# Softmax denominators of the first attention layer: sums of probability tiles moved to GpSimd, denominators formed after the next unit's first key tile

## The reference

```python
def _L0_conv_ref(x, w_proj, b_proj, w_out, b_out):
    B, C, H, W = x.shape                      # 8, 256, 32, 32
    N = H * W                                 # 1024 tokens
    tokens = x.reshape(B, C, N).transpose(0, 2, 1)
    qkv = (tokens @ w_proj + b_proj).reshape(B, N, 8, 3 * 32)
    q, k, v = jnp.split(qkv, 3, axis=-1)
    attn = jnp.einsum('bihd,bjhd->bijh', q, k) * 32 ** (-0.5)
    attn = jax.nn.softmax(attn, axis=2)
    res = jnp.einsum('bijh,bjhd->bihd', attn, v).reshape(B, N, 256)
    out = res @ w_out + b_out + tokens
    return out.transpose(0, 2, 1).reshape(B, C, H, W)
```

## Time and profile before

| what | value |
|---|---|
| time, median of 3 runs | 3152.33 us (3150.02 to 3154.6) |
| the profiled execution | 3150.14 us, its span 3148.4 us |
| mean granted TensorE clock, of full speed | 0.929 |
| PE / DVE / ACT / POOL busy | 85% / 70% / 41% / 21% |
| layer 0's four units in the fourth image | 1233.5 to 1360.5 us |

### The profile page before, as it was taken

One profiled execution on the slowest core, in us unless ns is written; L12 is line 12 of the kernel. 1 busy time (PEld: TensorE's weight loads), 2 busy tenths in 40 slices (PEclk: granted clock), 3 DMA queues, 4 the chain that ended last, 5 costly groups with the idle time before them and its releaser, 6 DMA issues.

```text
span 3148.4 us, 43492 instructions
## 1 busy us (share of the span) xinstructions
PE 2668.8 (85%) x14974; PEld 1865.5 (59%) x14974; DVE 2200.9 (70%) x2403; ACT 1287.3 (41%) x1860; POOL 656.9 (21%) x405
## 2 busy tenths in 40 slices
PE   6889979899788897888879888888888898888993
PEld 4447754577545775467654676447764477644772
DVE  4776668666686676867678566785668766777666
ACT  2553325433354333543335333453334533255333
POOL 0520116102160022500225002340024300252011
PEclk8999989999899998999989999899989999999997
DMA  6100050000400004000040001300022000310016
GB/s 151 27 24 1 0 128 1 24 1 14 115 1 24 1 14 115 1 24 1 23 106 1 24 1 42 87 1 24 1 64 65 24 1 1 92 38 24 1 54 240
DMA packets 46389, 124.58 MB, mean 40 GB/s; under 512 B 9792, under 2 KB 21312, under 8 KB 42560
## 3 DMA queue, kind: packets, MB, share of 16 engines
q1 hardware_dynamic: 46144, 121.41, 14.1%
HBM read 43.01 MB, written 23.86 MB: 21 GB/s over the span
## 4 chain that ended last, share of the span: by engine, by line
PE 59%; issue 13%; DVE 11%; ACT 4%; SPq 4%; POOL 4%; DMA 3%; DVEq 0%; ACTq 0%; POOLq 0%
PE tile L1352 23%; PE pv L1352 10%; POOL acc L619 4%; PE tile L1611 4%; PE tile L1430 4%; PE tile L1456 3%; SPq L518 3%; PE pv L1466 3%; DVE small L961 3%; PE tile L1486 2%; DMA stack<-qk_r 2%; PE tile L1633 2%; PE tile L1741 2%; PE tile L1660 1%; PE tile L1511 1%
## 5 line engine op out<-in xcount | busy, mean ns | idle before, releaser
L961 DVE TENSOR_REDUCE small<-tile 128x1 f32<-128x1024 f32 x512 | 598.3, 1216 | 116.9 <-PE tile L1430 116.7
L740 ACT ACTIVATE p<-tile 128x512 f32<-128x512 f32 (+1 forms) x640 | 411.0, 684 | 247.4 <-PE tile L1456 246.0
L1430 PE MATMUL tile<-stack 96*128 96x512 f32 x1024 | 368.1, 451 | 118.4 <-DVE small L961 45.6
L1352 PE MATMUL tile<-qk_r 128*128 128x512 f32 x1536 | 377.9, 395 | 0.0
L1430 PEld LDWEIGHTS tile<-stack 96*128 96x128 f32 x1024 | 180.5, 201 | 319.7 <-DVE small L961 111.8
L619 POOL TENSOR_TENSOR acc<-acc,p 128x1024 f32<-128x1024 f32 x144 | 359.1, 2518 | 1.9
L649 POOL TENSOR_TENSOR row_sum<-act 128x256 f32<-128x256 f32 x32 | 42.1, 1335 | 1498.3 <-DVE act L1187 1498.3
L1352 PEld LDWEIGHTS tile<-qk_r 128*128 128x128 f32 x1536 | 287.1, 188 | 66.7 <-issue 7.7
L1192 DVE TENSOR_TENSOR pl<-p,ph 128x1024 fp32r<-128x1024 f32 x128 | 158.3, 1236 | 238.2 <-ACT p L834 238.2
L1466 PE MATMUL pv<-p,v 128*32 128x512 f32 x2048 | 282.7, 626 | 1.4 <-ACT p L740 1.4
L1456 PE MATMUL tile<-stack 112*128 112x512 f32 x768 | 273.3, 424 | 10.8 <-DVE rec L1009 9.2
(11 more groups left out here) (285 smaller groups left out, 4541.4 us busy)
## 6 DMA issues: line engine op xcount, KB each, us to landing
stack<-qk_r SPq DMA_DIRECT2D x192, 256.0 KB, 5.0
x_in<-in_x_dram SPq DMA_DIRECT2D x9, 1024.0 KB, 7.5
act<-in_x_dram SPq DMA_DIRECT2D x8, 1024.0 KB, 8.0
x_scratch<-act SPq DMA_DIRECT2D x7, 1024.0 KB, 4.4
z_scratch<-zbuf SPq DMA_DIRECT2D x7, 1024.0 KB, 5.2
stack<-ones SPq DMA_DIRECT2D x8, 512.0 KB, 7.6
w3f<-w3f_scratch SPq DMA_DIRECT2D x8, 512.0 KB, 3.2
fin_rest<-z_scratch SPq DMA_DIRECT2D x3, 1024.0 KB, 12.9
```

What stands on the lines that cost most here:

```text
L740: sc.activation(p0[:, jt % DEPTH, pair, first:first + len(heads) * HALF], tile_wait(b, "st0", *u, jt, k), ACT.Exp, scale=float(D) ** -0.5) ...
L961: ve.tensor_reduce(maxima[:, h * NT + it:h * NT + it + 1], t[:], X, ALU.max).then_inc(vector_done, vector.one("max0", g, h, it))
L1352: ins = mm(out, lhs[a][kt_], rhs[c][kt_], start=first and kt_ == 0 and m == 0, stop=last and kt_ == n - 1 and m == 2)
L1430: ins = mm(o[:, s], stack[0:IMAX, 0, g, h, it * P:(it + 1) * P], stack[0:IMAX, 1, g, h, s], start=True, stop=True)
```

## The change

Five things are changed together, all in layer 0.

1. `adder`: GpSimd makes all ten sums of each unit with maxima; VectorE makes only those of the last unit. (`SUMMED_LAST` = 6 leaves the last unit's number of summed tiles as it was.)
2. `den0` of a unit with maxima moves from behind the unit's `m0` to behind the next unit's scores of key tile 0, and takes key tiles 6 and 7 first and `acc0` last. In the last unit it stands where it did, with the new inner order.
3. `rec0` and `rows0` move from key tile 0 to 1 of the next unit, `ex0` from 1 to 2, `res`, `res_hi` from 2 to 3, `res_lo` on GpSimd from behind the sums of key tile 1 to behind those of key tile 3, `out0(0)` from key tile 4 to 5 of the last unit, `x1(0)` from 5 to 6.
4. In key tiles 0 and 7 of the units with maxima both `s0` come ahead of the four `st0`.
5. `den0` of unit (1,0) takes its PSUM tile from the ring "whole". The exponentials no longer wait for `den0` by a semaphore of its own, since a later `st0` stands behind it. The wait for `max_cols` moves ahead of the whole `st0` tile.

```diff
-POOL_BOTH = (1, 2, 4)
+SUMMED_LAST = 6
+def summed(g, half):
+    return SUMMED_LAST if (g, half) == UNITS[-1] else SUMMED
 def adder(g, half, jt, pair):
-    if jt == 0 or jt >= SUMMED:
+    if jt == 0 or jt >= summed(g, half):
         return None
-    if (g, half) == UNITS[-1]:
-        return "vector"
-    return "pool" if pair == 0 or jt in POOL_BOTH else "vector"
+    return "vector" if (g, half) == UNITS[-1] else "pool"
...
-def key_tile(g, half):
+def key_tile(g, half, jt):
+    if next_unit(g, half) and jt in (0, NT - 1):
+        return ("s0", 0), ("s0", 1), ("st0", 0), ("st0", 1), ("st0", 2), ("st0", 3)
     if next_unit(g, half):
         return ("s0", 0), ("st0", 0), ("st0", 1), ("s0", 1), ("st0", 2), ("st0", 3)
     return ("st0", 0), ("st0", 1)
...
+            s += [("den0", *last_unit(*u))] if last_unit(*u) and jt == 0 else []
             s += [("pv0", *u, jt - 1)] if jt else []
-            s += [("ex0", *last_unit(*u))] if last_unit(*u) and jt == 1 else []
-            s += [("out0", 0)] if u == UNITS[-1] and jt == 4 else []
-        s += [("pv0", *u, NT - 1), ("m0", *next_unit(*u)), ("den0", *u)] if next_unit(*u) else (
+            s += [("ex0", *last_unit(*u))] if last_unit(*u) and jt == 2 else []
+            s += [("out0", 0)] if u == UNITS[-1] and jt == 5 else []
+        s += [("pv0", *u, NT - 1), ("m0", *next_unit(*u))] if next_unit(*u) else (
             [("den0", *u), ("pv0", *u, NT - 1)])
...
-        if kind in ("st0", "den0"):
+        if kind == "st0":
             looped = unit != UNITS[-1]
...
-        elif kind == "ex0":
+        elif kind in ("den0", "ex0"):
             looped = next_unit(*unit) not in (None, UNITS[-1])
...
-                    for jt in range(SUMMED - 1, NT):
-                        if jt >= SUMMED:
-                            scalar_wait(*exp_of(g, half, jt, 1))
-                        src = acc0[:, half] if jt < SUMMED else p0[:, jt % DEPTH]
+                    o, top = free("den0", g, half), summed(g, half)
+                    for jt in (*range(top, NT), top - 1):
+                        if jt >= top and (g, half) == UNITS[-1]:
+                            scalar_wait(*exp_of(g, half, jt, 1))
+                        elif jt >= top:
+                            pass
+                        elif (g, half) == UNITS[-1]:
+                            for pair in range(2):
+                                vector_wait("add0", g, half, jt, pair)
+                        else:
+                            for pair in range(2):
+                                pe.wait_ge(pool_done, gps.at(b, "add0", g, half, jt, pair))
+                        src = acc0[:, half] if jt < top else p0[:, jt % DEPTH]
```

More of the change, by code:

```diff
@@ L141, in scalar_steps @@
             s += [("exp0", *u, jt, k) for k in range(score_tiles(*u))]
-            s += [("res_hi", *last_unit(*u))] if last_unit(*u) and jt == 2 else []
+            s += [("res_hi", *last_unit(*u))] if last_unit(*u) and jt == 3 else []
     s += [("pv0_out", *UNITS[-1]), ("res_hi", *UNITS[-1])]
@@ L166, in vector_steps @@
         for jt in range(NT):
-            s += [("rec0", *last), ("rows0", *last)] if last and jt == 0 else []
-            s += [("res", *last)] if last and jt == 2 else []
-            s += [("x1", 0, ct) for ct in range(CT)] if u == UNITS[-1] and jt == 5 else []
+            s += [("rec0", *last), ("rows0", *last)] if last and jt == 1 else []
+            s += [("res", *last)] if last and jt == 3 else []
+            s += [("x1", 0, ct) for ct in range(CT)] if u == UNITS[-1] and jt == 6 else []
             for pair in range(2):
@@ L214, in pool_steps @@
     for u in UNITS:
-        for jt in range(1, SUMMED):
+        for jt in range(1, summed(*u)):
             s += [("add0", *u, jt, pair) for pair in range(2) if adder(*u, jt, pair) == "pool"]
-            s += [("res_lo", *last_unit(*u))] if last_unit(*u) and jt == 1 else []
+            s += [("res_lo", *last_unit(*u))] if last_unit(*u) and jt == 3 else []
     s += [("pool", k, ct) for k in range(10) for ct in range(CT)] + [("sm", 0)]
@@ L620, in _ @@
                                              ).then_inc(pool_done, gps.one("add0", *u, jt, pair))
-                        if jt == 1 and last_unit(*u):
+                        if jt == 3 and last_unit(*u):
                             g, half = last_unit(*u)
@@ L720, in _, with kept @@
                                   ID).then_inc(scalar_done, scalar.one("v0_kept", k))
-                def summed(u, jt, pair):
-                    if jt >= SUMMED:
-                        act_e.wait_ge(tensor_done, tensor.at(b, "den0", *u))
+                def kept(u, jt, pair):
+                    if jt >= summed(*u):
+                        assert tensor.place["den0", *u] < tensor.place["st0", *next_unit(*u), jt - DEPTH, 0]
                     elif adder(*u, max(jt, 1), pair) == "pool":
@@ L737, in exp0 @@
                         act_e.wait_ge(tensor_done, tensor.at(b, "pv0", *former[0], former[1]))
-                        summed(*former, pair)
+                        kept(*former, pair)
                     first = heads[0] % 2 * HALF
@@ L774, in _ @@
                             exp0(u, jt, k)
-                        if last and jt == 2:
+                        if last and jt == 3:
                             res_hi(*last)
@@ L1064, in _ @@
                     for jt in range(NT):
-                        if last and jt == 0:
+                        if last and jt == 1:
                             inverse0(last)
-                        elif last and jt == 2:
+                        if last and jt == 3:
                             normalise0(last)
-                        if not following and jt == 5:
+                        if not following and jt == 6:
                             x1(0)
@@ L1407, in vector_wait, with free @@
                     pe.wait_ge(vector_done, vector.at(b, *step))
-                def free(*name):
+                def free(*name, but=None):
                     for engine, count in leavers(b, *name):
+                        if engine == but:
+                            continue
                         pe.wait_ge(scalar_done if engine == "scalar" else vector_done, count)
@@ L1449, in st0 @@
                         scalar_wait("pv0_out", *last_unit(g, half))
-                    o = free("st0", g, half, jt, k)
-                    for q, h in enumerate(heads_of(g, half, k)):
+                    heads = heads_of(g, half, k)
+                    if jt == 0 and G // 2 in heads:
+                        scalar_wait("max_cols", g, half, HT - 1)
+                    o = free("st0", g, half, jt, k, but="scalar" if jt == 0 and G // 2 in heads and last_unit(g, half) else None)
+                    for q, h in enumerate(heads):
                         if jt == 0 and h < G // 2:
                             vector_wait("max_rows", g, half, h)
-                        elif jt == 0 and h == G // 2:
-                            scalar_wait("max_cols", g, half, HT - 1)
                         ins = mm(o[:, halves[q]], stack[0:K0, 1, g, h, jt * P:(jt + 1) * P],
@@ L1486, in den0 @@
                                 ins = mm(o[D * h:D * h + D, 0:P], seg, src[:, h // 2, i:i + P],
-                                         start=t == 0 and jt == SUMMED - 1, stop=t == HT - 1 and jt == NT - 1)
+                                         start=t == 0 and jt == top, stop=t == HT - 1 and jt == top - 1)
                     ins.then_inc(tensor_done, tensor.one("den0", g, half))
@@ L1537, in _ @@
                     for jt in range(NT):
-                        for kind, k in key_tile(*u):
+                        for kind, k in key_tile(*u, jt):
                             if kind == "st0":
@@ L1542, in _ @@
                                 s0(*rows_of(following, 2 * jt + k))
+                        if last and jt == 0:
+                            den0(*last)
                         if jt:
                             pv0(*u, jt - 1)
-                        if last and jt == 1:
+                        if last and jt == 2:
                             ex0(*last)
-                        if not following and jt == 4:
+                        if not following and jt == 5:
                             out0(0)
@@ L1551, in _ @@
                         m0(*following)
-                        den0(*u)
                     else:
```

8 lines of the change are left out of this document (1 added, 7 removed).

## The result

The changed kernel takes 3201.15 us (median of 4 runs, 3200.95 to 3201.57), the kernel before in the same comparison 3151.9 (3150.02 to 3154.6): ratio 1.0156, 95% interval 1.0138 to 1.0173. It is slower by 49 us where 88 us less were forecast. The profiled execution took 3200.95 us; its mean granted clock is 0.912 of full speed, against 0.929.

What follows compares the result with a forecast made beforehand. TensorE bounds plain key tiles, VectorE's sums stretch others and delay `m0`. Savings 2.9 + 3.5 + 3.5 + 1.1 = 11.0 us an image, 88 for eight, give 3064 us, 2.8% less; range 3040 to 3106.

Steps and rivals of the forecast that it cites:

- VectorE needs about 3.7 (0.7 to the first score tile, 2.34, and 0.6 for the negation): Unit's end: VectorE's time in us from the last key tile's start to `m0`, within an allowance of 4.5.
- Hidden: GpSimd's two added sums a unit cost nothing: they end 3.2 us behind `m0`'s start, 2.7 before `den0` needs `acc0`.
- rival B: Boundaries between units: TensorE's clock falls once `den0` no longer fills the spreading; 41 us, giving 3105; chance 0.11.
- 2.9 were to go: Unit (0,0): without VectorE's sums stretching tiles, `m0` starts at 1260.3 instead of 1263.25, 2.9 us less.
- 30.8 twice: Units (0,1) and (1,0): 30.8 us between starts of `m0`, against 34.4; 3.5 us less taken for each.
- 6.75, twice: Units (0,1) and (1,0): whole `den0` done, and key tile 1 starting, 6.75 us behind `m0`'s start.
- The last unit's 1.1 us less: Last unit: with `den0` in another PSUM tile, scores and exponentials come earlier, 1.1 us less an image.
- the 4.5 us from the last tile's start to the mark: Unit's end: 4.5 us from the last key tile's start to `m0`, VectorE's 3.7 plus allowance for TensorE's last `pv0`.
- rival A: Layer 0: GpSimd becomes the bound if its sums take 3.23 us each; 62 us slower, 3214; chance 0.08.
- The zero for the passage between images: Passage to the next image: the turned PSUM ring gains 0, within bounds of 0 and 7.8 us over the run.
- C: Key tiles 1 to 4: PSUM and VectorE queue behind the moved chain, 1 us more a unit, 3088; chance 0.15.
- E: Units' boundaries: nothing moves, as `den0` takes back in the open what the sums free; 3152; chance 0.03.

Runs made afterwards that it cites:

- two-input form: Changed kernel with layer 0's negation and copy on VectorE written as operations of two inputs, the second zeros: 3202.2 us, ratio 1.0152.
- the wait filled: Changed kernel with ten 96x512 matmuls that nobody reads ahead of `m0`'s wait for the negation, at three boundaries an image: 3147.87 us, ratio 0.9983.
- the schedule alone: Changed kernel with VectorE's two sums a unit given back (pair 1 of key tiles 3 and 5): 3229.71 us, ratio 1.0236.
- the sums alone: Kernel before with all sums of the units with maxima moved to GpSimd and nothing else: 3210.22 us, ratio 1.0172.
- fewer sums: Changed kernel with `SUMMED = 5` in the units with maxima, so eight sums a unit on GpSimd: 3100.2 us, ratio 0.983.
- the gap: Changed kernel, GpSimd waiting for the end of the negation before its last two sums of a unit: 3092.15 us, ratio 0.9805.

## Why the prediction was wrong

**The step that failed** is "VectorE needs about 3.7 (0.7 to the first score tile, 2.34, and 0.6 for the negation)", together with the verdict on GpSimd's two more sums, "Hidden". The 0.6 was right for a negation beside an idle GpSimd. In the kernel before, GpSimd had finished its eight sums by then; the two sums that were added lie exactly on the negation's time. They were counted against `den0` (slack 2.7 us, and `den0` indeed never waited for GpSimd), never against VectorE's small instructions, though the prediction's own sum has GpSimd busy until 3.2 us behind the mark, and so right across the negation in front of it. Measured: 11.0 us in the fourth image, 93 in the run.

The trace of before could have told. It has VectorE's sums at two prices, here in unit order: the six of one image's units with maxima, beside GpSimd; then the last unit's, without it; and of the first kind one with its neighbour.

```profile
L993 DVE TENSOR_TENSOR acc<-acc,p x6: 2730/3313/3405, 1249.6 to 1325.9; 128x1024 f32<-128x1024 f32 x6
...
L993 DVE TENSOR_TENSOR acc<-acc,p x8: 1210/1221/2319, 1344.3 to 1355.3; 128x1024 f32<-128x1024 f32 x8
...
1256.88 2.39 POOL L619 TENSOR_TENSOR acc<-acc,p 128x1024 f32<-128x1024 f32 x1
```

The sum of 3.40 us in the earlier trace rows starts 0.07 us behind GpSimd's, which ends at 1259.27; the sum ends at 1260.35, 1.08 later. It hadn't run slowly, it had been kept out for 2.3 us. The prediction took 3.40 as the price of a sum and read on. The Trainium skill says this in "SBUF — State Buffer", section "Who interferes with whom": VectorE and GpSimd share a port pair under an exclusive lock, whoever is first holds it for the whole instruction; `copy` and `tensor_scalar` can need it, operations with two SBUF inputs need it against an instruction of GpSimd that reads SBUF, and reductions don't on this chip. The trace agrees on all three sides: negation 4.1 us, two-input form 3.97, maxima 2.36 for two, as before. The trace adds that VectorE was kept out over more than one sum in a row (4.17 us against 2.34 for one). The prediction had cited the like rule, but asked only what VectorE does to GpSimd's sums, not what they do to VectorE.

**The clock** (rival B) was given 0.11 and 41 us, for a gap that was to shrink. The gap grew instead, since the first loss feeds the second: TensorE waits 2.2 to 3.1 us for the negation, then for the spreading without `den0` in between. The price: 9.0 and 9.5 us to key tile 1 against 7.08 with the wait filled, and from the last mark to the last reciprocal 28.8 against 26.9, so 1.9 + 2.4 + 1.9 = 6.2 an image, 50 in all. Filling the wait gave back 53. The argument against B was that 2.27 us of idling in front of `m0` had brought no slow tile. It looked at a wait with `den0`'s 96 matmuls right behind `m0`, and they were the part that the change moves: in the schedule alone a shorter wait, 1.80 us, is followed by the lower clock in all eight images, before in none. Length counts too: with `den0` in its old place and waits of 3.4 to 4.5 us (the sums alone) the clock was low at 19 of 24 boundaries.

**The account,** for the fourth image. From TensorE's first tile to the first mark 30.33 us; forecast 26.8, since before it was 29.68 and 2.9 were to go. Mark to mark 36.29 and 36.89; forecast 30.8 twice, before 34.4. Last mark to the last reciprocal 28.8; forecast 26.4, before 27.5. The misses are 3.5 + 5.5 + 6.1 + 2.4 = 17.5 us an image, 140 in all, against 3201 - 3064 = 137. The negation and the clock explain 11.0 + 6.2 = 17.2 of them.

That so little is left is partly luck, for smaller misses of both signs cancel. Key tiles 0 and 1 of unit (0,0) took 8.07 us, before 6.85, and nothing was put on it. Key tile 1 starts 7.08 us behind the mark even with the wait filled, where the forecast had 6.75, twice. The last unit's 1.1 us less came to half: 26.9 with the wait filled. Against these three, the 4.5 us from the last tile's start to the mark were too many: measured 6.86, 7.67 and 7.74, without the negation's loss 3.75, 3.74 and 3.74, three times 0.75 less. There the prediction's first figure for VectorE, 3.7, was right.

The other seven images are worse than the fourth, with marks 36.8 to 37.0 and 37.5 to 37.6 us apart. Over all eight, layer 0's stretch takes 133.3 us against 126.1 before, 57 more in all, of which the rest of the profiled execution gives back 7; where, was not looked into.

The two rows of before that bound its units, for the 29.68 (1263.25 - 1233.57) and the 27.5 (1359.50 - 1332.02):

```profile
1233.57 0.80 PE L1430 MATMUL tile<-stack 96*128 96x512 f32 x1 [6.08 <-ACT stack L748]
...
1359.50 0.96 DVE L1009 RECIPROCAL rec<-tile 128x128 f32<-128x128 f32 x1 [1.75 <-PE tile L1486]
```

**What was right.** The undisturbed tile of 3.08 us and its return in place of the tiles beside VectorE's sums; 2.38 us for a sum on GpSimd; rival A's bound never reached (its two thresholds are given the wrong way round: by its own 1250.0 + 30a against 1339.2 the gain is gone at a = 2.97, and GpSimd begins to decide at about 2.65). With the negation free, the marks are 31.39 to 33.07 us apart against 30.8, so the working of a unit stands, less the clock. The zero for the passage between images is right too: the first projection no longer waits, and the loads of `stack` are issued 1219.12 - 1210.92 = 8.2 us behind the store in front of them, before 1199.86 - 1191.60 = 8.3.

```profile
1209.66 0.62 PE L1358 MATMUL tile<-xh,w0h 128*128 128x512 f32 x2
...
1210.92 0.35 SPq L542 DMA_DIRECT2D z_scratch<-zbuf  x1
...
1219.12 28.80 SPq L523 DMA_DIRECT2D stack<-qk_r  x24
```

C didn't come. The tiles 1 to 4 of unit (0,1) take 3.27, 3.64 (with `ex0`), 3.47 and 3.08 us, by their starts in the changed kernel (1293.25, 1296.52, 1300.16, 1303.63, 1306.71).

E's form, that `den0` in the open takes back what the sums free, isn't what happened: with the negation free, the changed kernel gains 54 to 62 us (fewer sums, the gap).

## What to carry to other kernels

Before moving work to GpSimd, list every VectorE instruction that will lie beside it, above all the short ones on the critical path: one that needs the shared ports costs the rest of GpSimd's run of instructions and not its own length, which a trace shows as two engines' instructions that end together, or as one line with two prices. If amount or place can't keep the two apart, let GpSimd wait once for the short chain; here that wait was worth 109 us, what it gave back in clock included. Price a wait on TensorE with what follows it: where a second wait and short matmuls come behind, 2 to 3 us of standing still cost through the clock some 2 us more. When such a wait is filled, look at all the others again: the low stretch can turn up at the next one.

## What the hardware showed that was not expected

- VectorE's 0.17 us instruction on 128x16 elements lasted up to 4.17 us (5.08 with the sums alone) beside GpSimd's sums of 2.34 us, across the boundary between two of them; with a semaphore wait between the sums it came in after one at most.
- Ten matmuls of no use, 2.56 us in a wait, made a kernel of 3201 us 53 us faster through the granted clock; six more in another wait, where the clock had fallen at one of three boundaries of every image, moved the fall to the third boundary in all eight images and gained nothing.
